# Second attention of a four-sublayer network: one transpose for two heads, and weights times values in four 64x64 tiles

## The chip, the cores and the metric

The kernel runs on one core of one Trainium2 chip. The metric is the device time of one execution in microseconds. Engines are named TensorE (PE in the profile, PEld for its loading of stationary operands), VectorE (DVE), ScalarE (ACT), GpSimd (POOL) and SyncE (SP). "Stationary" is the operand loaded into the array, "moving" the one that streams through it.

## The reference

The network has, one after the other, a mixture-of-experts layer, a causal attention, the mixture of experts again, a quantised gated layer, a second attention and the quantised layer again. Only the second attention is touched here. It attends over the first axis of its input, which has four entries, for 1024 columns and 16 heads of 64:

```
s, b, f = src.shape                      # 4, 1024, 128
qkv = jnp.einsum('sbf,pf->sbp', src, in_proj_weight) + in_proj_bias
q, k, v = jnp.split(qkv, 3, axis=-1)     # each 16 heads x 64
attn = jax.nn.softmax(jnp.einsum('nsd,ntd->nst', q / np.sqrt(d), k), axis=-1)
out = jnp.einsum('nst,ntd->nsd', attn, v)
out = out.reshape(s * b, h * d) @ out_proj_weight.T + out_proj_bias
x = x + out
```

So each token attends to only four tokens, those of its own column.

## The kernel before

`attention1_stage` is a software pipeline written by hand. The 4096 tokens are 32 tiles of 128; four tiles (QT) make a window w, so there are 8 windows. A tile of 128 tokens is 2 groups of 64 (index g), and a group holds 4 positions of 16 columns: attention never leaves a group of 64.

A unit of work is one slot i = 8w + r. There are 64 units, and the stages of a unit lie in different slots, by the constants `L_QK, L_S, L_TURN, L_V, L_PV, L_OUT = 0, 1, 11, 11, 12, 13`. In slot i TensorE does, in this order of program:

- QK (L1227 by L1236 and L1238): queries and keys of a pair of heads (128 rows) for a window of 512 tokens, into `pq` and `pk`. Each is three products of the split type fp32r (high times high, low times high, high times low).
- TURN (L1245): `pm`, the softmax weights of eight heads of one tile spread over a 64-wide pattern with zeros, is transposed into `pT`: eight transposes of 128x128. In `pm` (L1407, GpSimd) each head has 128 columns, 64 for g = 0 and 64 for g = 1, and `mask2` sets those of the other group to zero.
- V (L1227 by L1255): values of eight heads for one tile of 128 tokens, 512 columns, into `pV`; tokens are the stationary side (`xsh`, `xsl`).
- OUT (L1265): output projection of eight heads, four fp32 products of 128x128, from `ab` into `pO`. The hardware makes two passes of each fp32 product, so the profile counts eight.
- S (L1277): scores, eight fp32 products with 64 stationary columns, each into its half of the partitions of `pS`: 16 passes.
- PV (L1289): weights times values. Eight fp32 products, one for each head: 128 rows (tokens of both groups) by 64 stationary columns (`vb`), 128 moving columns (`pt`), even heads into partitions 0 to 63 of `pA`, odd heads into 64 to 127: 16 passes.

ScalarE copies `pq` to `qb` with the bias (L1304), `pT` to `pt` (L1313, 1024 columns), `pA` to `ab` (L1318, 512 columns). In every slot with r = 2 it then copies the window's part of `xh` and `xl` to `xsh` and `xsl` (L1323), on which V of the next slot waits by `x_copied`. VectorE writes `kz` (L1338, two instructions of 64 partitions; zeros stand beside the keys so that one product gives two heads), copies `pV` to `vb` (L1343), multiplies the scores by `mask16` (L1350), sums them (L1362), adds `pO` to the residual X (L1357), and does the softmax once in eight slots (L1369 to L1381). GpSimd expands the weights to `pm` (L1407, two instructions, one for each g). All waits are counts of semaphores written out by hand; `need` is a wait. Buffers `qb`, `kz`, `vb`, `pm` and `pt` are double, `ab` and the PSUM tiles single.

Of the kernel before, what the change touches and what calls it, by code (L numbers as in the profile page):

```python
# [10 lines left out]
P = 128  # L11
D = 128
# [1158 lines left out]
def attention1_stage(nc, C, name, load):  # L1171
# [6 lines left out]
    X, ident, xh, xl, mask16, mask2 = C["X"], C["ident"], C["xh"], C["xl"], C["mask16"], C["mask2"]  # L1178
# [7 lines left out]
    with Scope(nc, name) as s:  # L1186
        qb = [s.sb(f"qb{u}", [P, W]) for u in range(2)]
        kz = [s.sb(f"kz{u}", [P, 2, W]) for u in range(2)]
# [3 lines left out]
        xsh, xsl = s.sb("xsh", [P, W], F32R), s.sb("xsl", [P, W], F32R)  # L1192
# [25 lines left out]
        with nc.Block() as block:  # L1218
            @block.tensor
            def _(pe):  # L1220
# [8 lines left out]

                def slot(w, r, on):  # L1230
# [8 lines left out]
                    if on(L_TURN):  # L1239
                        j = i - L_TURN  # L1240
                        need(pe, expanded, 2 * (j + 1))
                        need(pe, t_kept, j)
                        m = pm[(r - L_TURN) % 2][:, :, :, :, :].rearrange("p h g t b -> p (h g t b)")
                        for hh in range(8):
                            last = nc.tensor.transpose(pT[:, hh * P:(hh + 1) * P], m[:, hh * P:(hh + 1) * P], ident[:, :])  # L1245
                        last.then_inc(t_ready, 1)
                    if on(L_V):
                        j = i - L_V
                        rr = (r - L_V) % 8
                        gp, u = rr // 2, rr % 2  # L1250

                        need(pe, x_copied, 2 * (w - (1 if r >= L_V - 8 else 2) + 1))
                        need(pe, v_kept, j)
                        c0 = 2 * INNER1 + u * 512
                        split3(pV[:, :], slice(c0, c0 + 512), xsh[:, gp * P:(gp + 1) * P], xsl[:, gp * P:(gp + 1) * P], True).then_inc(v_ready, 1)  # L1255
                    if on(L_OUT):
                        j = i - L_OUT
                        rr = (r - L_OUT) % 8
                        gp, u = rr // 2, rr % 2
                        need(pe, a_kept, j + 1)  # L1260
                        if u == 0:

                            need(pe, o_added, 4 * (w - (1 if r >= L_OUT - 8 else 2)) + gp)
                        for c in range(4):
                            last = mm(pO[:, 0:D], ab[:, c * P:(c + 1) * P], Wt["wo"][:, (4 * u + c) * D:(4 * u + c + 1) * D],  # L1265
                                      start=(u == 0 and c == 0), stop=(u == 1 and c == 3))
                        last.then_inc(o_done, 1)
                    if on(L_S):
# [5 lines left out]
                        for gp in range(QT):  # L1274
                            for g in range(2):
                                o = gp * P + g * 64
                                last = mm(pS[g * 64:(g + 1) * 64, gp * P:(gp + 1) * P].rearrange("p (a k) -> p a k", a=2),  # L1277
                                          qb[par][:, o:o + 64], kz[par][:, :, o:o + 64],
                                          start=True, stop=True)
                        last.then_inc(s_ready, 1)  # L1280
                    if on(L_PV):
                        j = i - L_PV
                        par = (r - L_PV) % 2
                        need(pe, t_kept, j + 1)
                        need(pe, v_kept, j + 1)
                        need(pe, a_kept, j)
# [9 lines left out]
            def _(act):  # L1296
                a = nc.scalar

                def slot(w, r, on):
# [14 lines left out]
                    if on(L_PV):  # L1314
# [12 lines left out]
            def _(dve):  # L1327
# [3 lines left out]
                def slot(w, r, on):  # L1331
                    i = 8 * w + r
                    if on(L_QK):
                        need(dve, k_ready, i + 1)
                        need(dve, s_ready, i - 1)
                        for par in range(2):
                            o = slice(64 * par, 64 * par + 64)
                            v.tensor_scalar(kz[r % 2][o, par, :], pk[o, :], Wt["bqk"][o, CH1 + r:CH1 + r + 1], None, ALU.add).then_inc(k_kept, 1)  # L1338
# [34 lines left out]
                    if r == 1 and on(2):  # L1373
# [5 lines left out]
                        if not isinstance(w, int) or w > 1:  # L1379
                            need(dve, expanded, 16 * (w - 1))  # L1380
                        v.tensor_tensor(Pn[:, :, :], Ec[:, :, :], b(ri), ALU.mult).then_inc(p_ready, 1)  # L1381
                for u in range(2):
                    v.memset(kz[u][:, :, :], 0.0).then_inc(zeroed, 1)
# [8 lines left out]
            def _(pool):  # L1392
# [3 lines left out]
                def slot(w, r, on):  # L1396
                    i = 8 * w + r
                    if on(LE):
# [7 lines left out]
                        for gg in range(2):  # L1406
                            g.tensor_tensor(pm[rr % 2][:, :, gg, :, :].rearrange("p h t b -> p h t b"),  # L1407
                                            src.rearrange("p (h t) -> p h t", t=SEQ1).unsqueeze(3).to_broadcast([P, 8, SEQ1, PER]),
                                            mask2[:, gg * PER:(gg + 1) * PER].unsqueeze(1).unsqueeze(1).to_broadcast([P, 8, SEQ1, PER]),
                                            ALU.mult).then_inc(expanded, 1)  # L1410
# [688 lines left out]
```

## Time and profile before

| | |
|---|---|
| median of 3 runs | 2016.22 us (2015.75 to 2020.72) |
| the profiled execution | 2022.96 us, span 2021.2 us |
| TensorE busy | 1651.2 us (82%) |
| VectorE busy | 1333.7 us (66%) |
| ScalarE busy | 932.3 us (46%) |
| GpSimd busy | 654.2 us (32%) |
| second attention | about 1468 to 1865 us of the span |

The profile is of one execution. "Busy" is the time in which an engine executed; the spans of products are drawn longer than their spacing, because they are pipelined, so the distance from one start to the next is what tells their cost. Line numbers (L1245) are those of the kernel before.

### The profile page before, as it was taken

Reading aid. Unit: us, or ns where it says so; the run is one execution under the profiler, and the core shown is the slowest. Engines: PE = TensorE matmul, PEld = TensorE weight load, DVE = VectorE, ACT = ScalarE, POOL = GpSimd, SP = SyncE. Lnnn points to the kernel's source line nnn. Section 1 sums busy time; section 2 is a strip of 40 time slices with the busy share of each in tenths; the row PEclk is TensorE's granted clock in tenths of the full one; section 3 lists DMA queues with packets and bytes.
Section 4 is the critical chain, followed back from the end, with each engine's and each line's share of the span. In section 5 each row is a group of like instructions: output and inputs, shape, how many; then the busy total and the mean of one; then the engine's idle time right before and its main releaser. Section 6 shows DMA issues by size and latency. Waiting matters only on the chain. (4 is left out here: it accounts for less than half of the span.)

```text
span 2021.2 us, 31502 instructions
## 1 busy us (share of the span) xinstructions
PE 1651.2 (82%) x10385; PEld 1169.7 (58%) x10385; DVE 1333.7 (66%) x2565; ACT 932.3 (46%) x1650; POOL 654.2 (32%) x797
## 2 busy tenths in 40 slices
PE   2997783899999999997499778277489999998575
PEld 2666671655555555554466666155358888887354
DVE  5633455988787888782553345699786666662896
ACT  2323341488887888884333333133224444444232
POOL 2486454211111111111268545133213333333132
PEclk9999996999999999999599889699699999999798
DMA  6022321111111111110512232100100000000000
GB/s 230 25 66 63 112 58 66 31 33 30 33 28 27 37 27 37 27 27 7 196 35 67 64 101 60 49 1 0 43 1 1 1 0 0 0 0 1 0 0 42
DMA packets 47705, 82.34 MB, mean 41 GB/s; under 512 B 10948, under 2 KB 32900, under 8 KB 46532
## 3 DMA queue, kind: packets, MB, share of 16 engines
q1 hardware_dynamic: 38500, 62.09, 10.7%
q0 software_dynamic: 9088, 18.76, 2.8%
q8 instruction: 65, 1.06, 0.2%
q14 instruction: 52, 0.43, 0.1%
HBM read 43.19 MB, written 31.22 MB: 37 GB/s over the span
## 5 line engine op out<-in xcount | busy, mean ns | idle before, releaser
L1861 DVE TENSOR_REDUCE z_parts<-z_pM 128x4 f32<-128x512 f32 x576 | 373.4, 685 | 94.7 <-PE z_pM L1601 92.6
L1778 ACT ACTIVATE z_Pr<-z_pE 128x512 f32<-128x512 f32 x576 | 322.5, 596 | 89.6 <-PE z_pE L1625 86.9
L1625 PE MATMUL z_pE<-z_QM,z_QK 128*128 128x512 f32 x576 | 250.9, 438 | 11.3 <-DMA z_QM<-z_Q 8.7
L1965 POOL TENSOR_SCALAR_AFFINE_SELECT z_Pr<-z_Pr 128x512 f32<-128x512 f32 x128 | 81.2, 635 | 483.6 <-ACT z_Pr L1778 483.6
L1601 PE MATMUL z_pM<-z_KM,z_Q 128*128 128x512 f32 x576 | 232.0, 407 | 1.8 <-DVE z_Q L1851 0.9
L1407 POOL TENSOR_TENSOR a_pm<-a_Pn,k_mask 128x512 f32<-128x512 f32 x128 | 132.2, 1057 | 271.4 <-PE a_pT L1245 153.2
L1625 PEld LDWEIGHTS z_pE<-z_QM,z_QK 128*128 128x128 f32 x576 | 107.9, 188 | 162.4 <-ACT z_Pr L1778 91.7
L466 POOL DMA_INDIRECT slot_results<-m_yq,m_xq x156 | 153.6, 985 | 146.0 <-ACT m_yq L664 117.7
L439 POOL DMA_INDIRECT slot_rows<-m_XN,m_dest x128 | 126.6, 989 | 108.5 <-DVE m_dest L747 73.2
L1638 PE MATMUL z_pO<-z_Pr,z_V 128*9 128x512 f32 (+3 forms) x1536 | 159.6, 489 | 0.1
L800 DVE TENSOR_TENSOR m_h<-m_sg,m_gu 128x512 f32<-128x512 f32 x78 | 53.6, 687 | 110.1 <-ACT m_sg L656 90.0
L1338 DVE TENSOR_SCALAR a_kz<-a_pk,s_bqk 64x512 f32<-64x512 f32 x128 | 95.9, 749 | 44.4 <-PE a_pk L1227 41.9
L1601 PEld LDWEIGHTS z_pM<-z_KM,z_Q 128*128 128x128 f32 x576 | 108.7, 189 | 18.6 <-DVE z_parts L1861 3.3
L1318 ACT ACTIVATE a_ab<-a_pA 128x512 f32<-128x512 f32 x64 | 38.3, 598 | 147.5 <-PE a_pA L1289 147.5
L656 ACT ACTIVATE m_sg<-m_gu 128x512 f32<-128x512 f32 x78 | 46.6, 598 | 119.0 <-PE m_gu L560 106.9
L700 DVE TENSOR_TENSOR m_h<-m_sg,m_gu 128x512 f32<-128x512 f32 x64 | 44.0, 688 | 69.4 <-PE m_gu L484 47.2
L560 PE MATMUL m_gu<-s_wh,m_xqh 128*128 x156 | 73.8, 473 | 19.3 <-issue 16.5
L1313 ACT ACTIVATE a_pt<-a_pT 128x1024 f32<-128x1024 f32 x64 | 65.6, 1026 | 45.7 <-PE a_pT L1245 45.7
L1350 DVE TENSOR_TENSOR a_md<-a_pS,k_mask 128x512 f32<-128x512 f32 x64 | 44.3, 692 | 62.2 <-PE a_pS L1277 61.8
L636 ACT ACTIVATE m_sg<-m_gu 128x512 f32<-128x512 f32 x64 | 38.1, 599 | 90.6 <-PE m_gu L480 75.9
L1098 PE MATMUL f_op<-s_wdT,f_hT 128*128 128x128 f32 x384 | 54.0, 293 | 30.7 <-ACT f_hT L1044 30.7
L493 PE MATMUL m_po<-m_h,s_w 128*128 128x512 f32 x128 | 67.7, 611 | 7.3 <-DVE m_h L700 7.3
(290 smaller groups left out, 3815.3 us busy)
## 6 DMA issues: line engine op xcount, KB each, us to landing
slot_rows<-in_c_pad SPq DMA_DIRECT2D x2, 5070.0 KB, 24.0
m_xq<-slot_rows SPq DMA_DIRECT2D x38, 260.0 KB
z_QM<-z_Q SPq DMA_DIRECT2D x128, 64.0 KB, 2.0
z_KM<-z_QK SPq DMA_DIRECT2D x60, 128.0 KB, 2.4
m_raw<-in_gu SPq DMA_DIRECT2D x2, 2048.0 KB, 8.7
m_XN<-slot_results SPq DMA_DIRECT2D x8, 512.0 KB, 7.0
m_raw<-slot_results SPq DMA_DIRECT2D x8, 512.0 KB, 5.1
slot_results<-m_yq,m_xq POOLq DMA_INDIRECT x156
```

Source lines behind the costliest of these rows:

```text
L439: g_.indirect_dma_start(xs_dram, bass.IndirectOffsetOnAxis(dest[:, k, t:t + 1], 0), XN[:, t, 2 - XO[k]:2 - XO[k] + ROW], None).then_inc(se ...
L466: g_.indirect_dma_start(y_dram, bass.IndirectOffsetOnAxis(xq[q % RING][:, j % QT, TAG[list_of(j)]:TAG[list_of(j)] + 1].bitcast(I32), 0), y ...
L493: mm(po[:, :], w2[:, o:o + D], h[n % 2][:, :], start=(i == 0), stop=(i == NCHUNK - 1)).then_inc(h_used, 1)
L560: last = mm(gu[r % 2][:, u, :], xv[q % 2][:, c], wt[:, bass.ds(es[u] * GU, GU)], start=a, stop=b)
L1338: v.tensor_scalar(kz[r % 2][o, par, :], pk[o, :], Wt["bqk"][o, CH1 + r:CH1 + r + 1], None, ALU.add).then_inc(k_kept, 1)
L1407: g.tensor_tensor(pm[rr % 2][:, :, gg, :, :].rearrange("p h t b -> p h t b"), src.rearrange("p (h t) -> p h t", t=SEQ1).unsqueeze(3).to_br ...
L1601: last = mm(pM[n % 3][:, :].rearrange("p (h k) -> p h k", h=4), Q[G % 2][:, qt * P:(qt + 1) * P], KM[G % 2][:, :, kb * P:(kb + 1) * P], st ...
L1625: mm(pE[e % 2][:, :].rearrange("p (h c) -> p h c", h=4), QK[G % RING][:, kt * P:(kt + 1) * P], QM[half][:, :, q * P:(q + 1) * P], start=Tr ...
L1638: last = mm(pO[32 * h:32 * h + DH0 + 1, lo:512], V[:, (G // 4) * KT + kt, 4 * (G % 4) + h, :], Pr[j % 4][:, h, lo:512], start=(kt == 0), s ...
L1778: a.activation(Pr[j % 4][:, :, q * P:(q + 1) * P], pE[e % 2][:, :].rearrange("p (h c) -> p h c", h=4), ACT.Exp, scale=DH0 ** -0.5).then_in ...
L1861: v.tensor_reduce(parts[:, qt, kb, :], pM[n % 3][:, :].rearrange("p (h k) -> p h k", h=4), AX.X, ALU.max).then_inc(maxed, 1)
L1965: g_.affine_select(blk, blk, [[0, 4], [1, P]], ALU.is_ge, 0.0, base=0, channel_multiplier=-1).then_inc(selected, 1)
```

## The change

The softmax weights of a head are no longer spread over 128 columns with zeros for the other group. `pm` has 64 columns a head, so a transpose of 128 columns turns two heads side by side: four transposes instead of eight, one GpSimd instruction instead of two, and `pt` and `pT` are half as wide. After the transpose the even head of a pair lies in partitions 0 to 63 and the odd head in 64 to 127, for g = 0 in columns 0 to 63 and g = 1 in 64 to 127. To make the contraction rows fit, the scores of g = 1 have odd and even head exchanged (new layout of `kz`), and the values of odd heads are computed with the two halves of the tokens exchanged: `xsh` and `xsl` get 192 columns a tile, the last 64 a copy of the first, and V becomes two times three products of 256 columns. PV becomes sixteen products of 64 rows by 64 stationary columns with 64 moving columns, in the four 64x64 tiles of the array; the two halves of rows write to two PSUM tiles `pA[0]` and `pA[1]`. `ab` is filled by four copies of 64x256 instead of one of 128x512. The waits of PV stand ahead of S.

```diff
-        pm = [s.sb(f"pm{u}", [P, 8, 2, SEQ1, PER]) for u in range(2)]
-        pt = [s.sb(f"pt{u}", [P, 8 * P]) for u in range(2)]
-        ab = s.sb("ab", [P, 4 * P])
-        pq, pk, pS, pV, pA, pO = (s.ps(n, [P, 512]) for n in ("pq", "pk", "pS", "pV", "pA", "pO"))
-        pT = s.ps("pT", [P, 1024])
+        pm = [s.sb(f"pm{u}", [P, 8, SEQ1, PER]) for u in range(2)]
+        pt = [s.sb(f"pt{u}", [P, 4 * P]) for u in range(2)]
+        ab = s.sb("ab", [P, 4, 2, 64])
+        pq, pk, pS, pV, pT, pO = (s.ps(n, [P, 512]) for n in ("pq", "pk", "pS", "pV", "pT", "pO"))
+        pA = [s.ps(f"pA{u}", [P, 512]) for u in range(2)]
...
+                def values(out, u, odd, x_hi, x_lo):
+                    cols = lambda wt: wt[:, 2 * INNER1 + u * 512:2 * INNER1 + (u + 1) * 512].rearrange("p (i k c) -> p i k c", k=2, c=DH1)[:, :, odd, :]
+                    mm(out, x_hi, cols(Wt["wh"]), start=True, stop=False)
+                    mm(out, x_lo, cols(Wt["wh"]), start=False, stop=False)
+                    return mm(out, x_hi, cols(Wt["wl"]), start=False, stop=True)
...
-                        for hh in range(8):
+                        for hh in range(4):
                             last = nc.tensor.transpose(pT[:, hh * P:(hh + 1) * P], m[:, hh * P:(hh + 1) * P], ident[:, :])
...
-                        split3(pV[:, :], slice(c0, c0 + 512), xsh[:, gp * P:(gp + 1) * P], xsl[:, gp * P:(gp + 1) * P], True).then_inc(v_ready, 1)
+                        for odd in range(2):
+                            xr = slice(64 * odd, 64 * odd + P)
+                            last = values(pV[:, odd * 256:(odd + 1) * 256].rearrange("p (i c) -> p i c", c=DH1), u, odd, xsh[:, gp, xr], xsl[:, gp, xr])
+                        last.then_inc(v_ready, 1)
...
+                    if on(L_PV):
+                        j = i - L_PV
+                        need(pe, t_kept, j + 1)
+                        need(pe, v_kept, j + 1)
+                        need(pe, a_kept, 4 * j)
                     if on(L_S):
...
-                        for hh in range(8):
-                            h0 = (hh % 2) * 64
-                            last = mm(pA[h0:h0 + 64, (hh // 2) * P:(hh // 2 + 1) * P], vb[par][:, hh * 64:(hh + 1) * 64],
-                                      pt[par][:, hh * P:(hh + 1) * P], start=True, stop=True)
+                        for c in range(4):
+                            for g in range(2):
+                                for odd in range(2):
+                                    half = (g + odd) % 2
+                                    rows, o = slice(64 * half, 64 * half + 64), odd * 256 + c * 64
+                                    last = mm(pA[half][64 * odd:64 * odd + 64, c * 64:(c + 1) * 64], vb[par][rows, o:o + 64],
+                                              pt[par][rows, c * P + g * 64:c * P + g * 64 + 64], start=True, stop=True)
...
-                        a.activation(ab[:, :], pA[:, :], ACT.Copy).then_inc(a_kept, 1)
+                        for half in range(2):
+                            for odd in range(2):
+                                rows = slice(64 * odd, 64 * odd + 64)
+                                a.activation(ab[rows, :, (half + odd) % 2, :], pA[half][rows, 0:256].rearrange("p (c k) -> p c k", c=4), ACT.Copy).then_inc(a_kept, 1)
...
-                            a.activation(dst[:, :], src[:, bass.ds((w - 1) * W, W)].bitcast(F32), ACT.Copy).then_inc(x_copied, 1)
+                            of = src[:, bass.ds((w - 1) * W, W)].bitcast(F32).rearrange("p (g k) -> p g k", g=QT)
+                            a.activation(dst[:, :, 0:P], of, ACT.Copy).then_inc(x_copied, 1)
+                            a.activation(dst[:, :, P:P + 64], of[:, :, 0:64], ACT.Copy).then_inc(x_copied, 1)
...
-                            v.tensor_scalar(kz[r % 2][o, par, :], pk[o, :], Wt["bqk"][o, CH1 + r:CH1 + r + 1], None, ALU.add).then_inc(k_kept, 1)
+                            v.tensor_scalar(kz[r % 2][o, :, par:4 - par:3 - 2 * par, :], pk[o, :].rearrange("p (n g k) -> p n g k", n=QT, g=2), Wt["bqk"][o, CH1 + r:CH1 + r + 1], None, ALU.add).then_inc(k_kept, 1)
...
-                        for gg in range(2):
-                            g.tensor_tensor(pm[rr % 2][:, :, gg, :, :].rearrange("p h t b -> p h t b"),
...
+                        g.tensor_tensor(pm[rr % 2][:, :, :, :], src.rearrange("p (h t) -> p h t", t=SEQ1).unsqueeze(3).to_broadcast([P, 8, SEQ1, PER]),
+                                        mask16[:, :].unsqueeze(1).unsqueeze(1).to_broadcast([P, 8, SEQ1, PER]), ALU.mult).then_inc(expanded, 1)
```

The counts in the other waits follow (`expanded` one instead of two a unit, `a_kept` four instead of one, `x_copied` four instead of two a window).

## Rows read from the trace of the kernel before

**Rows 1.** The page's first part: busy time, share of the span, instructions.

```profile
PE 1651.2 (82%) x10385; PEld 1169.7 (58%) x10385; DVE 1333.7 (66%) x2565; ACT 932.3 (46%) x1650; POOL 654.2 (32%) x797
```

**Rows 2.** Stretches, full slots and tail: us; PE, PEld, DVE, ACT, POOL busy; PEclk; DMA.

```profile
1515.12:1818.43 303.31, 303.31 (x2909) 265.98 (x2907) 196.97 (x311) 125.94 (x171) 105.43 (x102) 1.00 0.00 0
1818.43:1865.00 46.57, 44.46 (x435) 39.04 (x433) 13.35 (x25) 20.27 (x27) 18.61 (x18) 1.00 0.01 1
```

**Rows 3.** Order of time, one full slot on PE: start, length, line, operation.

```profile
1604.35 0.50 PE L1227 MATMUL a_pq<-s_xh,s_wh 128*128 x1
...
1605.15 0.40 PE L1227 MATMUL a_pk<-s_xh,s_wh 128*128 x1
...
1605.85 1.03 PE L1245 MATMUL a_pT<-k_ident,a_pm 128*128 128x128 f32 x8
1606.64 0.48 PE L1227 MATMUL a_pV<-s_wh,a_xsh 128*128 128x512 f32 x1
...
1607.42 1.05 PE L1265 MATMUL a_pO<-s_wo,a_ab 128*128 128x128 f32 x8
1608.40 1.09 PE L1277 MATMUL a_pS<-a_kz,a_qb 128*64 128x128 f32 x16
1609.33 1.04 PE L1289 MATMUL a_pA<-a_pt,a_vb 128*64 128x128 f32 x16
1610.30 0.50 PE L1227 MATMUL a_pq<-s_xh,s_wh 128*128 x1
```

**Rows 4.** Order of time, first attention: 128-column products of the split type.

```profile
378.37 0.28 PE L1585 MATMUL z_pE<-s_wh,s_xl 128*128 128x128 f32 x1
378.48 0.28 PE L1585 MATMUL z_pE<-s_wl,s_xh 128*128 128x128 f32 x1
```

**Rows 5.** Order of time, first attention: eight passes in four column tiles.

```profile
502.74 0.41 PE L1638 MATMUL z_pO<-z_Pr,z_V 128*9 128x128 f32 x8
503.07 0.50 PE L1625 MATMUL z_pE<-z_QM,z_QK 128*128 128x512 f32 x1
```

**Rows 6.** Order of time on DVE, the slot after a softmax; [idle before <-releaser].

```profile
1597.65 0.69 DVE L1350 TENSOR_TENSOR a_md<-a_pS,k_mask 128x512 f32<-128x512 f32 x1 [0.90 <-PE a_pS L1277]
```

**Rows 7.** Groups by form: busy us, mean ns of one, idle before.

```profile
L1313 ACT ACTIVATE a_pt<-a_pT 128x1024 f32<-128x1024 f32 x64 | 65.6, 1026 | 45.7 <-PE a_pT L1245 45.7
L1033 ACT ACTIVATE f_xT<-f_txp 128x256 f32<-128x256 f32 x32 | 12.3, 384 | 59.9 <-PE f_txp L1072 59.9
L1308 ACT ACTIVATE a_Ec<-a_Dc 128x256 f32<-128x256 f32 x8 | 3.3, 417 | 1.3 <-DVE a_Dc L1372 1.3
L1407 POOL TENSOR_TENSOR a_pm<-a_Pn,k_mask 128x512 f32<-128x512 f32 x128 | 132.2, 1057 | 271.4 <-PE a_pT L1245 153.2 <-DVE a_Pn L1381 118.2
```

**Rows 8.** Order of time, the slot r = 3 of a window (with copies of x).

```profile
1598.52 0.60 ACT L1318 ACTIVATE a_ab<-a_pA 128x512 f32<-128x512 f32 x1 [2.47 <-PE a_pA L1289]
1599.02 0.62 ACT L1323 ACTIVATE a_xsh<-s_xh 128x512 fp32r x1
1599.54 0.62 ACT L1323 ACTIVATE a_xsl<-s_xl 128x512 fp32r x1
```

**Rows 9.** Order of time on PE in the tail, starts of groups.

```profile
1825.56 1.09 PE L1289 MATMUL a_pA<-a_pt,a_vb 128*64 128x128 f32 x16
...
1827.43 0.48 PE L1227 MATMUL a_pV<-s_wh,a_xsh 128*128 128x512 f32 x1
...
1829.20 1.09 PE L1289 MATMUL a_pA<-a_pt,a_vb 128*64 128x128 f32 x16
1830.23 1.09 PE L1245 MATMUL a_pT<-k_ident,a_pm 128*128 128x128 f32 x8
1832.03 0.50 PE L1227 MATMUL a_pV<-s_wh,a_xsh 128*128 128x512 f32 x1 [0.71 <-ACT a_xsl L1323]
...
1859.32 1.09 PE L1289 MATMUL a_pA<-a_pt,a_vb 128*64 128x128 f32 x16
1861.12 1.16 PE L1265 MATMUL a_pO<-s_wo,a_ab 128*128 128x128 f32 x8 [0.70 <-ACT a_ab L1318]
```

More of the change, by code:

```diff
@@ L1187, in attention1_stage @@
         qb = [s.sb(f"qb{u}", [P, W]) for u in range(2)]
-        kz = [s.sb(f"kz{u}", [P, 2, W]) for u in range(2)]
+        kz = [s.sb(f"kz{u}", [P, QT, 4, 64]) for u in range(2)]
         md = s.sb("md", [P, 4 * 2 * SEQ1, PER])
@@ L1191, in attention1_stage @@
         mx, sm, ri = (s.sb(n, [P, QT * HEADS1]) for n in ("mx", "sm", "ri"))
-        xsh, xsl = s.sb("xsh", [P, W], F32R), s.sb("xsl", [P, W], F32R)
+        xsh, xsl = s.sb("xsh", [P, QT, 3 * 64], F32R), s.sb("xsl", [P, QT, 3 * 64], F32R)
         vb = [s.sb(f"vb{u}", [P, W]) for u in range(2)]
-        pm = [s.sb(f"pm{u}", [P, 8, 2, SEQ1, PER]) for u in range(2)]
-        pt = [s.sb(f"pt{u}", [P, 8 * P]) for u in range(2)]
-        ab = s.sb("ab", [P, 4 * P])
-        pq, pk, pS, pV, pA, pO = (s.ps(n, [P, 512]) for n in ("pq", "pk", "pS", "pV", "pA", "pO"))
-        pT = s.ps("pT", [P, 1024])
+        pm = [s.sb(f"pm{u}", [P, 8, SEQ1, PER]) for u in range(2)]
[3 more added lines that the diff above has]
+        pA = [s.ps(f"pA{u}", [P, 512]) for u in range(2)]
         q_ready, k_ready, q_kept, k_kept, s_ready, masked, reduced = (
@@ L1250, in slot @@
                         gp, u = rr // 2, rr % 2
-                        need(pe, x_copied, 2 * (w - (1 if r >= L_V - 8 else 2) + 1))
+                        need(pe, x_copied, 4 * (w - (1 if r >= L_V - 8 else 2) + 1))
                         need(pe, v_kept, j)
-                        c0 = 2 * INNER1 + u * 512
-                        split3(pV[:, :], slice(c0, c0 + 512), xsh[:, gp * P:(gp + 1) * P], xsl[:, gp * P:(gp + 1) * P], True).then_inc(v_ready, 1)
+                        for odd in range(2):
+                            xr = slice(64 * odd, 64 * odd + P)
+                            last = values(pV[:, odd * 256:(odd + 1) * 256].rearrange("p (i c) -> p i c", c=DH1), u, odd, xsh[:, gp, xr], xsl[:, gp, xr])
+                        last.then_inc(v_ready, 1)
                     if on(L_OUT):
@@ L1259, in slot @@
                         gp, u = rr // 2, rr % 2
-                        need(pe, a_kept, j + 1)
+                        need(pe, a_kept, 4 * (j + 1))
                         if u == 0:
@@ L1264, in slot @@
                         for c in range(4):
-                            last = mm(pO[:, 0:D], ab[:, c * P:(c + 1) * P], Wt["wo"][:, (4 * u + c) * D:(4 * u + c + 1) * D],
+                            last = mm(pO[:, 0:D], ab[:, c, :, :].rearrange("p g k -> p (g k)"), Wt["wo"][:, (4 * u + c) * D:(4 * u + c + 1) * D],
                                       start=(u == 0 and c == 0), stop=(u == 1 and c == 3))
                         last.then_inc(o_done, 1)
+                    if on(L_PV):
[3 more added lines that the diff above has]
+                        need(pe, a_kept, 4 * j)
                     if on(L_S):
@@ L1283, in slot @@
                         par = (r - L_PV) % 2
-                        need(pe, t_kept, j + 1)
-                        need(pe, v_kept, j + 1)
-                        need(pe, a_kept, j)
-                        for hh in range(8):
-                            h0 = (hh % 2) * 64
-                            last = mm(pA[h0:h0 + 64, (hh // 2) * P:(hh // 2 + 1) * P], vb[par][:, hh * 64:(hh + 1) * 64],
-                                      pt[par][:, hh * P:(hh + 1) * P], start=True, stop=True)
+                        for c in range(4):
[5 more added lines that the diff above has]
+                                              pt[par][rows, c * P + g * 64:c * P + g * 64 + 64], start=True, stop=True)
                         last.then_inc(pv_ready, 1)
```

15 lines of the change are left out of this document (6 added, 9 removed).

## The prediction

> **What bounds the kernel now.** I read the engines' totals, then the busy times by stretch, then the order of time inside one slot. Over the whole kernel TensorE is busy 82% [rows 1], a mean over stages with different limits, so the stage decides. Its steady part is 51 equal slots (i = 13 to 63) from 1515.12 to 1818.43 us: TensorE is busy 303.31 of 303.31 us, at a granted clock of 1.00 (the 2.4 GHz level), VectorE 197 us, ScalarE 126 us [rows 2]. One slot takes 1610.30 - 1604.35 = 5.95 us, and TensorE works through it in the order pq, pk, pT, pV, pO, pS, pA without an idle gap [rows 3]. So a slot costs what its groups cost, start to start:
>
> pq 0.80, pk 0.70, pT 0.79, pV 0.78, pO 0.98, pS 0.93, pA 0.97, together 5.95 us [rows 3].
>
> Two things inside these numbers are needed below. A 128x128 load with a 128-column product takes 0.11 us: eight transposes in 0.79, eight pO passes in 0.98 less 0.10. Where the array goes from 128x128 to 128x64 or back, about 0.10 us is lost ahead of it (pO: 0.98 against 8 x 0.11; pA: 0.97 against eight pairs at 0.109, 0.87), and the first load behind it is not hidden (pq 0.80 against pk 0.70; pS 0.93 against 0.87) [rows 3]. pA already runs in two column tiles: 16 passes of 128 columns in 8 pairs.
>
> The Trainium skill (TensorEngine Tiling, "Key Properties") says that a change of the tiling mode drains the engine; by that rule the new step from 128x64 (pS) to 64x64 (pA) costs as much as the ones above, and I charge 0.10 for it. It speaks against this change; without it the slot would be 0.10 shorter.
>
> **The change, part by part, on TensorE.**
> TURN: four transposes instead of eight, 4 x 0.11 = 0.44 less: pT 0.35.
> V: three products of 512 columns become six of 256. Three of 512 take 0.70 in pk, 0.233 each [rows 3], so 256 columns are 0.115. The bound by the weights is 0.11: full loads with 128-column products of this split type come every 0.11 us [rows 4]. Both say 6 x 0.115 = 0.69, and 0.69 is what three of 512 are in pV too (0.78 less 0.09 for a first product that is charged longer). Taken: 0.78 unchanged (0.75 to 0.85).
> OUT and S keep instruction counts and shapes. S's new layout of keys only makes its moving rows contiguous: nothing. S is followed by a change of mode: pS 0.93 + 0.10 = 1.03.
> PV: 16 products in two passes each, 32 passes of 64 rows by 64 columns in four tiles. Between the ends: if all four tiles run at once, 8 rounds of 64 columns at 0.109/2 = 0.055 are 0.44, with 0.05 for the first load and 0.10 for the change of mode 0.59 us. If the two halves of rows don't run beside each other, or loads of 64 columns aren't hidden behind products of 64, it is 16 steps of 0.055, 0.87 + 0.15 = 1.02. No operation with 64 rows is in the trace. The nearest row is the first attention's pO: eight passes in four column tiles, 128 columns, 0.33 us start to start with the change behind it, so two rounds of 0.11 and not eight [rows 5]. Four tiles in parallel are shown, row halves are not. I take 0.59.
> The waits of PV are moved ahead of S. They ask for t_kept, v_kept and a_kept of the slot before, all a slot old or needed by OUT already, so S does not wait for them. Cost nothing.
> New slot: 0.80 + 0.70 + 0.35 + 0.78 + 0.98 + 1.03 + 0.59 = 5.23, 0.72 us less.
>
> **On the other engines.** VectorE: the same instructions (the two writes of kz get another stride, the element count stays); in the fullest slot (softmax) it still waits 0.90 us for pS ahead of md [rows 6], more than the slot loses, 0.72. Cover just holds. GpSimd: one instruction of 1.06 us instead of two [rows 7], hidden before and after. ScalarE: pt is 128x512 instead of 128x1024, near the 0.60 of pA's copy instead of 1.03 [rows 7, 8]. But pA's copy becomes four of 64x256. A copy of 256 from PSUM lasts 0.384 [rows 7]; back to back, copies start about 0.10 before the one ahead ends (0.60 long, 0.50 apart; 0.62 long, 0.52 apart) [rows 8], so 0.28 each and 1.24 for four instead of 0.60. In a full slot OUT needs them 2.63 us in: hidden.
>
> **Where that cover is gone.** Once in 8 slots ScalarE copies xsh and xsl between ab and qb. Before: ab starts 0.11 into slot r=3 (1598.52 against 1598.41), xsl ends at 1600.16, 1.75 in; V starts 2.29 in [rows 3, 8] and doesn't wait. After: ab from 0.11, four steps of 0.284 to 1.25, then 0.52 and 0.31 (256 from SBUF: 0.417 [rows 7] less 0.10) for xsh, 0.52 and 0.41 for xsl: x_copied at 3.01, with 0.05 for the semaphore 3.06. V would start at 0.80 + 0.70 + 0.35 = 1.85. TensorE stands still 1.2 us, with OUT, S and PV queued behind that wait. Bounds: 1.0 (64 rows cheaper) to 1.8 (no overlap of the copies). Six of the 51 slots are such slots.
>
> **Head and tail of the stage.** Slots 0 to 10 have no changed group. Slots 11 and 12 gain 0.44 and 0.72. In the tail (no pq, pk) a slot is 3.64 us (1829.20 - 1825.56), of it pA 1.03 (1830.23 - 1829.20) and pT 0.84 (1827.43 - 1825.56 less 1.03) [rows 9]. After: pT 0.41 (0.84 less four times 0.11) and pV 0.78 end at 1.19, but OUT now waits for the four copies, 0.22 + 1.24 = 1.46; then pO 0.98, pA 0.65 (0.59, and 0.06 that pA has more in the tail now, 1.03 against 0.97): 3.09, 0.55 less in eight slots, 4.4 us; slot 64 (with S) 0.45 less. The slot with the x copies: V starts at 3.06 instead of 1.80 (1832.03 against 1830.23, a wait of this kind is there already [rows 9]) and is 0.84 longer. The last two distances from PV to OUT, 1.79 (0.97 for pA, 0.60 for the copy, 0.22 between) [rows 9], become 0.59 + 1.46 = 2.05, 0.26 more each; one of them stands against a turn that is 0.22 shorter. Net tail: 4.4 + 0.45 - 0.84 - 0.3 = 3.7.
>
> **Sum.** 51 x 0.72 = 36.7; slots 11 and 12 1.2; x copies 6 x 1.2 = 7.2 lost; tail 3.7: 34.4 us less. The profiled execution took 2022.96 (span 2021.2), the median of the three runs is 2016.22; the sum is a difference inside the span and nothing around it moves, so I take it from the median: 2016.2 - 34.4 = 1981.8, say 1982.
>
> **Rivals.**
> (a) Row halves in turn, or loads not hidden: PV 1.02 instead of 0.59. 0.43 x 64 = 27.5 more: 2009. For it: no row with 64 rows. Against: column tiles run side by side both in loads and products [rows 3, 5]. Chance 0.09.
> (b) A floor for each matmul, whatever its width. From rows: the eight passes in 0.33 less 0.10 are 0.029 apart on average [rows 5], so nothing denser is shown over a group; 32 x 0.029 + 0.15 = 1.08 at the worst, 0.49 more than taken, at the best nothing. Halfway (0.022 each, 0.85) it is 0.26 x 64 = 17 more: 1999. Chance 0.12.
> The Trainium skill (TensorE: Matmul & The Clock Gate, "Wait — 56ns, not 53.3ns?") states such a floor: start to start never below about 25 ns. Estimate from that page: 32 x 0.025 = 0.80, PV 0.95, about 2005. No row here settles whether it holds across tiles; rows 5 show eight passes within 0.33 us.
> (c) Slower: instructions can't be supplied. Load and product count each. Per slot TensorE executes (2909 + 2907) / 51 = 114 now [rows 2]; the densest stretch is pS and pA, 64 in 1.90 us, 0.030 each [rows 3]. After, the same stretch has 96 in 1.62 us, 0.017 each. If 0.030 is the sustained limit, it takes 2.88, 1.26 more: the slot is 6.49, 0.54 longer than before; in the tail 64 x 0.030 is 1.92 for PV, 1.33 more than taken in 12 slots, 16 less the gain of 3.7. 51 x 0.54 + 7.2 + 12 = 47 more than before: 2063. It decides from 0.023 an instruction ((1.62 + 0.58) / 96; 0.58 is the slot's gain after its share of the x copies, 7.2 / 51). Against it: the 0.030 is explained by the columns alone. Chance 0.07.
> (d) ScalarE's small copies cost more, or VectorE's cover of 0.18 us in the softmax slots fails: x stalls of 1.8 and half a us in two slots of eight, 4 + 6 = 10 more: 1992. Chance 0.10.
> That the change doesn't do what it says: half the transposes and half of GpSimd's instructions go in any case, so this is (a).
>
> **How the numbers follow.** Forecast 1982: chance 0.62, its own range 1973 (S to PV without the 0.10, stalls of 1.0) to 1990. (a) 0.09, (b) 0.12, (c) 0.07, (d) 0.10. Range 1972 to 2006: it takes in the forecast, (d) and (b), together 0.84; (a) and (c) stay outside. A measurement of this kernel can tell about 0.3%, 6 us, from no change. Faster by more, under 2010: forecast, (d), nearly all of (b) and most of (a): 0.88. Within: 0.05. Slower: 0.07.
>
> **What would show it.** pT 0.35 and pV 0.78 start to start; pS 1.03 and pA 0.59 (0.59 right, 0.85 to 1.08 rival b, 1.02 rival a, 1.9 rival c); slot 5.23; a_ab's four copies 0.28 apart; in six slots TensorE idle about 1.2 us ahead of pV, released by ScalarE's a_xsl; in the tail a short wait of pO for a_ab. The prediction is wrong if pA's group is over 0.9 us, if TensorE waits in ordinary slots for VectorE or ScalarE, or if the granted clock in the stage falls from 1.00.

## The result and the profile after

The changed kernel takes 2001.71 us (median of 4; 2000.59 to 2003.37) against 2016.85 for the kernel before: ratio 0.9926, 95% interval 0.9911 to 0.9941, so 12 to 18 us faster. On a second chip it was 0.9911 (0.9888 to 0.9934). The forecast was 1982, with 1972 to 2006 as the range. The kernel is faster, as forecast, and the time lies inside the range, but the gain is 15 us where 34 were forecast.

The page of the profiled execution of the changed kernel: totals, then the groups on ScalarE and GpSimd that the change touches.

```profile
PE 1617.2 (81%) x11340; PEld 1139.1 (57%) x11345; DVE 1333.3 (67%) x2565; ACT 963.5 (48%) x1858; POOL 589.2 (29%) x733
...
L1343 ACT ACTIVATE a_ab<-a_pA 64x256 f32<-64x256 f32 x256 | 96.9, 379 | 151.4 <-PE a_pA L1311 146.7
L1433 POOL TENSOR_TENSOR a_pm<-a_Pn,k_mask 128x512 f32<-128x512 f32 x64 | 67.3, 1057 | 312.8 <-PE a_pT L1258 191.0
```

TensorE is 34 us less busy, GpSimd 65, and ScalarE 31 more: one copy of 0.60 (64 of them, 38.3 us) has become four of 0.379 (96.9 us), while the copy of `pT` to `pt` fell from 1.03 to 0.59. Lines have moved: TURN is now L1258, V L1239 to L1241, OUT L1280, S L1298, PV L1311, the copies of pA L1343.

One full slot on TensorE in the changed kernel, order of time:

```profile
1517.23 0.50 PE L1232 MATMUL a_pq<-s_xh,s_wh 128*128 128x512 f32 x1
...
1518.05 0.40 PE L1232 MATMUL a_pk<-s_xh,s_wh 128*128 128x512 f32 x1
...
1518.75 0.60 PE L1258 MATMUL a_pT<-k_ident,a_pm 128*128 128x128 f32 x4
1519.10 0.37 PE L1239 MATMUL a_pV<-s_wh,a_xsh 128*128 128x256 f32 x1
...
1519.88 1.05 PE L1280 MATMUL a_pO<-s_wo,a_ab 128*128 128x128 f32 x8
1520.86 1.09 PE L1298 MATMUL a_pS<-a_kz,a_qb 128*64 128x128 f32 x16
1521.89 0.70 PE L1311 MATMUL a_pA<-a_pt,a_vb 64*64 64x64 f32 x32
1522.51 0.50 PE L1232 MATMUL a_pq<-s_xh,s_wh 128*128 128x512 f32 x1
```

From start to start, beside [rows 3]: pq 0.82 (0.80), pk 0.70 (0.70), pT 0.35 (0.79), pV 0.78 (0.78), pO 0.98 (0.98), pS 1.03 (0.93), pA 0.62 (0.97). The slot is 5.28 us instead of 5.95, the forecast said 5.23.

The stretches that answer to [rows 2]: the 51 full slots, then the tail up to the last pO.

```profile
1511.98:1792.22 280.24, 271.10 (x3677) 234.40 (x3672) 196.65 (x311) 149.72 (x336) 53.70 (x51) 1.00 0.00 0
1792.22:1842.00 49.78, 39.26 (x615) 34.21 (x607) 13.50 (x26) 28.42 (x68) 9.45 (x9) 0.92 0.01 2
```

TensorE is no longer busy all of the time: 9.1 us are missing in the full slots. The sum of the prediction, part by part, against the two profiled executions (differences of starts of the first pq, of slots 13 and 64 and of the last pO; us):

| part | before | forecast | after |
|---|---|---|---|
| slots 0 to 12 | 46.6 | -1.2 | 45.6 (-1.0) |
| 51 full slots | 303.3 | -29.5 | 280.3 (-23.1) |
| tail to the last pO | 45.6 | -3.7 | 49.7 (+4.1) |
| the stage | 395.5 | -34.4 | 375.5 (-20.0) |

Ahead of the stage lie 1468.5 and 1466.4 us, behind its last pO 157.2 and 159.7 us. In ten other executions of this study the time ahead was anything between 1460.4 and 1473.9 us, whatever the second attention did, while the parts of the stage repeated within 0.2 us between the two executions of the changed kernel. The stage's own parts are therefore the measure below, and medians the check. The 2.5 us more behind the last pO are taken up under "The medians".

Where the 9.1 us went: a slot with r = 3, in order of time, both engines.

```profile
1543.63 0.50 PE L1232 MATMUL a_pq<-s_xh,s_wh 128*128 x1
...
1543.77 1.59 ACT L1343 ACTIVATE a_ab<-a_pA 64x256 f32<-64x256 f32 x4 [2.49 <-PE a_pA L1311]
...
1545.15 0.60 PE L1258 MATMUL a_pT<-k_ident,a_pm 128*128 128x128 f32 x4
...
1545.39 0.63 ACT L1349 ACTIVATE a_xsh<-s_xh 128x512 fp32r x1
...
1545.92 0.40 ACT L1350 ACTIVATE a_xsh<-s_xh 128x256 fp32r x1
1546.23 0.61 ACT L1349 ACTIVATE a_xsl<-s_xl 128x512 fp32r x1
1546.75 0.40 ACT L1350 ACTIVATE a_xsl<-s_xl 128x256 fp32r x1
...
1547.20 0.39 PE L1239 MATMUL a_pV<-s_wh,a_xsh 128*128 128x256 f32 x1 [1.45 <-ACT a_xsl L1350]
```

This is the wait that the prediction named, with its price wrong: pV starts 2.05 us after pT instead of 0.35, so 1.70 us are lost, not 1.2 (the whole slot takes 7.00 us, 1.72 more than 5.28). The prediction's upper bound for this wait, 1.8, was the one for copies that do not overlap. The copies of x behave as forecast (0.53, 0.31, 0.52 from start to start); the four copies of pA take 1545.39 - 1543.77 = 1.62 up to the start of the next copy, not 1.14.

The tail, order of time on TensorE:

```profile
1800.65 0.37 PE L1239 MATMUL a_pV<-s_wh,a_xsh 128*128 128x256 f32 x1
...
1802.01 1.16 PE L1280 MATMUL a_pO<-s_wo,a_ab 128*128 128x128 f32 x8 [0.42 <-ACT a_ab L1343]
1803.10 0.69 PE L1311 MATMUL a_pA<-a_pt,a_vb 64*64 64x64 f32 x32
1803.72 0.66 PE L1258 MATMUL a_pT<-k_ident,a_pm 128*128 128x128 f32 x4
1807.28 0.58 PE L1239 MATMUL a_pV<-s_wh,a_xsh 128*128 128x256 f32 x1 [2.90 <-ACT a_xsl L1350]
...
1837.40 1.73 PE L1280 MATMUL a_pO<-s_wo,a_ab 128*128 128x128 f32 x8 [1.70 <-ACT a_ab L1343]
```

From pV to pO are 1.36 us (0.78 before), and pO itself is 1.09 long, because its first load stands behind a wait. The slot with the x copies has pV 3.56 us behind pT. After this idle time TensorE's granted clock is lower:

```profile
1804.00:1812.00 8.00, 5.10 (x57) 4.57 (x56) 0.69 (x1) 4.38 (x11) 1.05 (x2) 0.79 0.00 0
1836.00:1844.00 8.00, 4.87 (x48) 4.16 (x48) 0.00 (x0) 2.79 (x8) 0.00 (x0) 0.61 0.00 0
```

Behind the wait of 2.90 us the mean over 8 us is 0.79, and the products of 256 columns start 0.21 us apart where they had been 0.115. Behind the last waits for `ab` it is 0.61.

### The profile page after: what moved, and what is told of

Same layout as the page of the kernel before. It is cut to its first block and busy times, and to the rows that moved or that the text cites. A ratio compares the mean times of both kernels' runs of the same rounds, so it can differ in the third digit from the quotient of the medians.

```text
span 2001.6 us, 33649 instructions
## 1 busy us (share of the span) xinstructions
PE 1617.2 (81%) x11340; PEld 1139.1 (57%) x11345; DVE 1333.3 (67%) x2565; ACT 963.5 (48%) x1858; POOL 589.2 (29%) x733
## 5 line engine op out<-in xcount | busy, mean ns | idle before, releaser
L1343 ACT ACTIVATE a_ab<-a_pA 64x256 f32<-64x256 f32 x256 | 96.9, 379 | 151.4 <-PE a_pA L1311 146.7
L1433 POOL TENSOR_TENSOR a_pm<-a_Pn,k_mask 128x512 f32<-128x512 f32 x64 | 67.3, 1057 | 312.8 <-PE a_pT L1258 191.0
L656 ACT ACTIVATE m_sg<-m_gu 128x512 f32<-128x512 f32 x78 | 46.6, 597 | 120.8 <-PE m_gu L560 120.8
L1280 PE MATMUL a_pO<-s_wo,a_ab 128*128 128x128 f32 x512 | 70.9, 283 | 7.6 <-ACT a_ab L1343 7.6
L1791 ACT ACTIVATE z_pM<-k_after_query 128x512 f32<-128x512 bf16 x120 | 72.6, 605 | 0.6 <-DVE z_parts L1885 0.5
```

What stands on the lines that cost most here:

```text
L1343: a.activation(ab[rows, :, (half + odd) % 2, :], pA[half][rows, 0:256].rearrange("p (c k) -> p c k", c=4), ACT.Copy).then_inc(a_kept, 1)
L1791: a.activation(pM[n % 3][:, :], after_query[:, :], ACT.Copy).then_inc(filled, 1)
```

## Experiments

The theory after reading the trace: TensorE's own sum is right, and what is missing is ScalarE. The four copies of 64x256 are not overlapped and end late; this makes V wait once a window, and OUT wait in each slot of the tail. Rivals: the x wait only hides another one; the number of copies does not matter; the four tiles are not what made PV short.

### x copies ahead of the copies of pA

```diff
+                    if r == L_V - 9 and on(L_V - 1):
+                        ...
+                            a.activation(dst[:, :, 0:P], of, ACT.Copy).then_inc(x_copied, 1)
+                            a.activation(dst[:, :, P:P + 64], of[:, :, 0:64], ACT.Copy).then_inc(x_copied, 1)
                     if on(L_PV):
...
-                    if r == L_V - 9 and on(L_V - 1):
-                        ...
```

> The changed kernel with one edit: in the slot r = 2 ScalarE copies xsh and xsl after pt and ahead of the copies of pA, not behind them. Theory (the loss against the forecast is the wait of V for x_copied, and in the tail what hangs on it): the wait of 1.72 us ahead of pV goes in all six full slots, 51 full slots take 280.3 - 10.3 = 270 us, the slot with the x copies in the tail falls from 7.48 to about 3.5 us, no stretch of the tail is at the lower clock; in all 14 us less than the changed kernel, about 1987. Rival (the x copies only move the wait: now they hold up the copies of pA, and OUT waits): the wait reappears ahead of pO and less than 4 us is gained, about 1999.

Measured: 1982.72 us against 2020.30 of the kernel before on this chip, ratio 0.9824 (0.9802 to 0.9846). The stretches of full slots and tail:

```profile
1506.44:1776.27 269.83, 269.46 (x3679) 234.10 (x3673) 196.63 (x311) 149.87 (x336) 53.80 (x51) 1.00 0.00 0
1776.27:1821.23 44.96, 36.79 (x612) 31.91 (x607) 13.47 (x26) 28.24 (x68) 9.46 (x9) 1.00 0.01 2
```

The full slots lose 10.4 us and TensorE is busy all but 0.4 us; the tail loses 4.7 and its clock is 1.00 throughout. The slot with the x copies in the tail takes 3.75 us (7.48 before the edit). The stage takes 360.3 us, 15.2 less than in the changed kernel, where 14 were expected. The theory stands and the rival falls: nothing waits in ordinary slots in place of V. The copies fit into time in which ScalarE had waited for pA, behind pt:

```profile
1535.16 0.59 ACT L1335 ACTIVATE a_pt<-a_pT 128x512 f32<-128x512 f32 x1
1535.76 0.63 ACT L1341 ACTIVATE a_xsh<-s_xh 128x512 fp32r x1
...
1537.12 0.40 ACT L1342 ACTIVATE a_xsl<-s_xl 128x256 fp32r x1
1538.23 1.59 ACT L1350 ACTIVATE a_ab<-a_pA 64x256 f32<-64x256 f32 x4 [0.72 <-PE a_pA L1311]
```

### The same edit in the kernel before

The edit is as above, with the two copies of 512 columns ahead of the one copy of pA.

> The kernel before with the one edit that helped the changed kernel: x copies ahead of the copy of pA. Theory (the wait in the full slots is made by the change; before, x_copied was 0.5 us early): full slots stay 303.3 us, the tail loses its one wait of 0.96 us, 44.6 instead of 45.6. Rival (the order helps any version by making the copy of pA or of pq fall better): the full slots fall under 302.

Measured: full slots 303.32 us, tail 44.59 (45.57 before the edit); one execution of 2019.22 us, the kernel before on this chip 2015.47 in the median. The order of the copies gains nothing in the full slots of the kernel before, and the 1.0 us of its one wait in the tail. So the wait in full slots is made by the change.

### Four copies in the kernel before

```diff
-                        a.activation(ab[:, :], pA[:, :], ACT.Copy).then_inc(a_kept, 1)
+                        for half in range(2):
+                            for odd in range(2):
+                                rows, cols = slice(64 * odd, 64 * odd + 64), slice(256 * half, 256 * half + 256)
+                                a.activation(ab[rows, cols], pA[rows, cols], ACT.Copy).then_inc(a_kept, 1)
```

> The kernel before with one part of the change alone: pA is copied to ab by four instructions of 64x256 instead of one of 128x512. Theory (copies of 64x256 don't overlap, 1.61 us in all): x_copied comes at 2.92 in its slot, V waits 0.6 us in six full slots, in the tail pO waits 0.2 us a slot, the last two distances from PV to OUT grow by 1.0 each: 3.7 + 2 + 2 + 1 = about 9 us slower, 2026. Rival (they overlap as forecast, 0.28 apart): x_copied at 2.4, 0.1 to 0.2 us in six slots and 1.3 at the end, 2 to 3 us slower, 2019.

Measured: 2027.02 us, ratio 1.0036 (1.0022 to 1.0051). Full slots 307.39 us (+4.1), tail 51.64 (+6.1). In its slot r = 3 pV starts 1.43 us after pT, 0.64 later than before, which is the 0.6 expected. In the stage this one part of the change costs the kernel before some 10 us (6.7 by the medians, 2027.02 against 2020.30), and the price without overlap is the right one: with overlap 2 to 3 us were expected.

### Two copies of 64x512

The counts in the waits for `ab` follow (two instead of four).

```diff
-        pA = [s.ps(f"pA{u}", [P, 512]) for u in range(2)]
+        pA = s.ps("pA", [P, 2, 512])
...
-                        for half in range(2):
-                            for odd in range(2):
-                                rows = slice(64 * odd, 64 * odd + 64)
-                                a.activation(ab[rows, :, (half + odd) % 2, :], pA[half][rows, 0:256]...
+                        for odd in range(2):
+                            rows = slice(64 * odd, 64 * odd + 64)
+                            dst = ab[rows, :, :, :] if odd == 0 else ab[rows, :, ::-1, :]
+                            a.activation(dst.rearrange("p c g k -> p g c k"), pA[rows, :, 0:256].rearrange("p h (c k) -> p h c k", c=4), ACT.Copy).then_inc(a_kept, 1)
```

> The changed kernel with pA as one tensor of two banks and two copies of 64x512 into ab instead of four of 64x256. Theory (each copy costs 0.40 us from start to start, its length and a gap of 0.02, none of it overlapped): two copies of 0.62 are 1.24 instead of 1.61, the wait ahead of pV falls from 1.72 to about 1.35, pV to pO in the tail from 1.36 to about 1.0; 6 x 0.37 + 12 x 0.37 = 6.6 us less than the changed kernel, about 1995. Rival (64-wide copies overlap once they are 512 long, as the 128-wide did, 0.50 apart): 1.10 for both, about 1993. Rival (the cost is by partitions and elements alone, the number of copies doesn't matter): no gain, 2002.

Measured: 1992.80 us, ratio 0.9863 (0.9839 to 0.9887). A copy is 0.592 long and the next starts 0.62 after its start: no overlap at 512 columns either (second copy and what follows, order of time on ScalarE):

```profile
1544.68 0.59 ACT L1343 ACTIVATE a_ab<-a_pA 64x512 f32<-64x512 f32 x1
1545.30 0.63 ACT L1349 ACTIVATE a_xsh<-s_xh 128x512 fp32r x1
```

Full slots 277.81 us (-2.4), tail 43.62 (-6.1), pV to pO in the tail 0.99. The full slots gain what was expected (6 x 0.37 = 2.2); the tail gains more than 12 x 0.37 = 4.4, and its mean granted clock is 0.96 instead of 0.92. So the number of copies matters: two of 512 columns take 1.23 us to the start of what follows, four of 256 take 1.62.

### Two copies of all 128 partitions

The four copies become two of 128x256, from pA[0] and pA[1]. The exchange of groups for odd heads is left out, so this kernel computes another attention and only its times are of use.

> The changed kernel with two copies of 128x256 from pA[0] and pA[1] into ab instead of four of 64x256; the exchange of the two groups for odd heads is left out, so the second attention's result is another one. It tells what forbids the overlap. If it is the 64 partitions: the two copies start 0.28 to 0.30 us apart. If it is the short length, 256 elements out of PSUM: they start 0.40 apart. In both cases the pair ends 0.8 to 0.9 us earlier than the four did, so the wait ahead of pV falls to about 0.9 and the total to about 1990.

Measured: the pair takes 0.66 us, each 0.38 long, so the second starts 0.28 after the first:

```profile
1545.83 0.66 ACT L1341 ACTIVATE a_ab<-a_pA 128x256 f32<-128x256 f32 x2 [2.59 <-PE a_pA L1311]
```

With 256 columns out of PSUM copies do overlap, if they are 128 wide. The wait ahead of pV is 0.63, where 0.9 was expected. The full slots take 273.73 us (-6.5) and the tail 37.57 (-12.1). The one execution took 1990.74 us, as expected, but with 1473.9 us ahead of the stage, the most of all. But the two copies of 64 differ from these in two things, in having 64 partitions and in changing them. The next run parts the two.

### The same four copies in another order

```diff
-                        for half in range(2):
-                            for odd in range(2):
+                        for odd in range(2):
+                            for half in range(2):
```

> The changed kernel with the order of the four copies of 64x256 changed: both of partitions 0 to 63, then both of 64 to 127. What forbids the overlap? If it is the change of partitions from one copy to the next: the first and second, and the third and fourth, start 0.28 us apart, the second and third 0.40; V's wait falls by 0.24. If it is that a copy has 64 partitions at all: all 0.403 apart, the same time as the changed kernel.

Measured: 1988.51 us in one execution; full slots 278.50 (-1.8), tail 45.12 (-4.6). The four copies together:

```profile
1544.36 1.32 ACT L1343 ACTIVATE a_ab<-a_pA 64x256 f32<-64x256 f32 x4 [2.43 <-PE a_pA L1311]
1545.71 0.69 ACT L1326 ACTIVATE a_qb<-a_pq,s_bqk 128x512 f32<-128x512 f32 x1
```

They take 1.32 us instead of 1.59: starts at 0.28, 0.67 and 0.96 after the first. So 64 partitions do not forbid the overlap. Going to other partitions than the copy ahead does; there 0.39 pass between the starts. It is not the PSUM tile that decides: the pairs that overlap here read one from pA[0] and one from pA[1], while in the changed kernel the first two copies read the same tile and do not overlap. Whether it is the partitions read or the partitions written stays open, as both change together. The stage takes 369.1 us, 6.2 less than in the changed kernel on this chip; the rest of the difference between the totals lies outside it. The order in the changed kernel alternates between partitions 0 to 63 and 64 to 127 at each step, the worst there is.

The Trainium skill (ScalarE: Activation LUTs, "What ACT_TABLE_LOAD costs") says that ACTIVATEs back to back overlap by about 93 ns. That agrees with the copies of equal partitions here (0.38 long, 0.28 apart). For a change of partitions the measurement decides: no overlap.

### PV tile by tile

```diff
-                        for c in range(4):
-                            for g in range(2):
-                                for odd in range(2):
+                        for g in range(2):
+                            for odd in range(2):
+                                for c in range(4):
```

> The changed kernel with the sixteen products of PV in another order: all four of one tile of the array, then the next tile, instead of one product for each of the four tiles in turn. Theory (the four tiles run beside each other only where products for different tiles stand next to each other in the queue; passes of one tile follow at 0.0585 us): 32 passes take 1.87 us, pA's group 2.0 instead of 0.62, a slot 6.65 instead of 5.28, and the total about 70 + 18 = 88 us more, near 2090. Rival (the array reorders, or the row halves do not matter and a pass is simply 0.0146 us): pA's group stays at 0.62.

Measured: 2050.92 us in one execution, 31 us over the kernel before on this chip (2020.08). Order of time on TensorE:

```profile
1559.49 1.54 PE L1311 MATMUL a_pA<-a_pt,a_vb 64*64 64x64 f32 x32
1560.95 0.50 PE L1232 MATMUL a_pq<-s_xh,s_wh 128*128 x1
```

The same 32 passes take 1.46 us instead of 0.62. So the four tiles are what made PV short, row halves included, and only because neighbours in the queue belong to different tiles. The 2.0 expected was too much, and with it the 88 us: the passes of two tiles that follow each other in the queue still overlap in part. The full slots take 321.47 us, 41 more, and the whole stage 51 more, so the order of these loops decides whether the change gains or loses.

### Both edits, and the changed kernel again beside them

> The changed kernel with both edits: x copies ahead of the copies of pA, and two copies of 64x512 instead of four of 64x256. Theory (the two losses are separate: the x wait in six full slots and one of the tail, the copies in every slot of the tail): 51 full slots 269.8 us as with the first edit alone, the tail 44.96 less 12 x 0.37 = 40.5 us, so some 4.5 us less than with the first edit alone and 14 to 15 less than the changed kernel in the stage's own time. Rival (the gains of the two edits overlap, both work on the same wait): no more than 1 us under the first edit alone, tail at 44.

> The changed kernel unaltered, on the same chip as the run with both edits, to compare the two and to see how much of the time lies outside the stage. Theory: the stage's parts repeat (0 to 12: 45.6, 13 to 63: 280.3, tail 49.7 us within 0.3), while the time ahead of the stage differs by some us from one execution to the next. Rival: the parts of the stage vary too, and the differences read between traces are partly chance.

Measured on one chip, the kernel before 2020.08: the changed kernel 2002.53, ratio 0.9911 (0.9888 to 0.9934); with both edits 1981.16, ratio 0.9804 (0.9782 to 0.9826). The parts of the changed kernel repeat (45.5, 280.3, 49.5 us). With both edits the full slots and the tail are:

```profile
1508.27:1778.03 269.76, 269.44 (x3678) 234.01 (x3673) 196.67 (x311) 137.92 (x234) 53.83 (x51) 1.00 0.00 0
1778.03:1818.07 40.04, 36.80 (x612) 31.91 (x607) 13.48 (x26) 23.94 (x42) 9.47 (x9) 1.00 0.01 2
```

The gains add: the tail is another 4.9 us shorter than with the first edit alone, where 4.5 was expected. By the ratios alone (0.9824 and 0.9804, intervals overlapping) the second edit could not be told from nothing; the parts of the stage show it. The stage takes 355.3 us, 40 less than before the change, where the changed kernel has 20 less.

### One of the two copies on VectorE

```diff
+                    if on(L_PV):
+                        j = i - L_PV
+                        need(dve, pv_ready, j + 1)
+                        need(dve, o_done, j)
+                        v.tensor_copy(ab[64:128, :, ::-1, :].rearrange("p c g k -> p g c k"), pA[64:128, :, 0:256].rearrange("p h (c k) -> p h c k", c=4)).then_inc(b_kept, 1)
                     if r == 0 and on(1):
```

> The kernel with both edits, and one more: of the two copies of 64x512 out of pA ScalarE keeps the one of partitions 0 to 63, VectorE takes the other, behind its sum of the scores in the same slot. Theory (in the tail pO waits for the copies alone: 0.99 us from pV to pO, 1.09 for pO and 2.02 from pA to pO twice): with both copies side by side 0.78, 0.98 and 1.4; the tail falls from 40.0 to about 35.5 us, the full slots keep 5.28 (269.8 us), near 1977. Rival (VectorE, busy 197 of 280 us and in order, becomes late in the slots with the softmax): TensorE waits for VectorE in full slots, over 272 us for the 51, and nothing is gained.

Measured: 1976.70 us, ratio 0.9813 (0.9789 to 0.9837) against 2015.47 on its chip, within the interval of both edits alone.

```profile
1508.16:1779.90 271.74, 270.92 (x3678) 234.48 (x3673) 233.78 (x362) 108.36 (x183) 53.82 (x51) 1.00 0.00 0
1779.90:1817.48 37.58, 34.34 (x612) 31.38 (x607) 22.61 (x39) 15.97 (x29) 9.45 (x9) 1.00 0.01 2
```

Both sides were half right: the tail gains 2.5 us, and the full slots lose 2.0, one slot in eight growing from 5.28 to 5.60 (5.76 once), where VectorE's copy comes late behind the softmax. The profile names no releaser for that wait of pO; the copy ends at 1585.29 and the first load of pO starts at 1585.53, so the copy as its cause is inferred from the times. The sum is 0.5 us. The version with both edits is simpler and as good.

## Why the prediction was right or wrong

**TensorE's sum: right.** pT 0.35, pV 0.78, pO 0.98 and pS 1.03 came as forecast, the last with the 0.10 for the new change of tiling mode; in that the trace agrees with the rule of the Trainium skill (TensorEngine Tiling, "Key Properties") that was cited. pA is 0.62 for 0.59, and pq 0.82 for 0.80. Together 0.05 a slot, 2.6 us in 51.

**Rival (a), row halves in turn: false.** pA would be 1.02; the run tile by tile shows what a lack of concurrency costs. **Rival (b), a floor for each pass: false** across tiles. 32 passes in 0.62 us, with 0.15 for the mode in it, are 0.015 each. The floor of 0.025 that the Trainium skill states (TensorE: Matmul & The Clock Gate, "Wait — 56ns, not 53.3ns?") would have given 0.80 for the passes alone; across tiles the measurement decides. **Rival (c), supply of instructions: false** as a price for each slot. It may show in one place: in the last slot of a turn of TensorE's loop, five times in the 51 slots, pA to pq takes 0.76 to 0.81 instead of 0.62.

```profile
1615.21 0.69 PE L1311 MATMUL a_pA<-a_pt,a_vb 64*64 64x64 f32 x32
1616.02 0.49 PE L1232 MATMUL a_pq<-s_xh,s_wh 128*128 x1
```

Before, the same place took 0.97 like any other. That the branch and the register instructions of the loop are no longer hidden behind a PV that is so short is the likely cause. The run tile by tile speaks for it: with as many instructions in the loop and a PV of 1.46 us, these slots are as long as the others (6.10). It was not tried by itself. The slots behind them are a little shorter, so that it costs 0.7 us in all.

**The step that failed** is the sentence "back to back, copies start about 0.10 before the one ahead ends ..., so 0.28 each". It carried an overlap over from rows of 128 partitions [rows 8] to copies that change partitions, where it is not there: 0.403 each. The mechanism (V waits for x_copied, OUT waits in the tail) was right, the term was mis-sized: 1.59 us for the four instead of 1.24. The run with the same four copies in another order shows that the change of partitions is what it missed. In the full slots 1.72 us were lost instead of 1.2, six times 0.52 = 3.1 us; with 2.6 for the slots and 0.7 for the loop that makes the 6.4 us that are missing there.

**The tail, +4.1 instead of -3.7,** failed by the same term and two that were not in the sum. From start to start (us):

- The copies, 4.3: pV to pO is 1.36 instead of 1.05 in ten slots (3.1), V starts 3.56 behind pT instead of 3.06 in the slot with the x copies (0.5), and the last two distances from pA to pO are 0.35 longer each for them (0.7).
- A pO whose first load stands behind a wait is 1.09 long, not 0.98, eleven times: 1.2. The first full wait of that kind could be read in the kernel before (1.16 for the group in [rows 9] against 1.05 in [rows 3]) and was not charged.
- The fallen clock, 2.5: behind its V the slot with the x copies takes 3.92 instead of 2.40 (7.48 in all instead of 5.46), and at the end a pO takes 1.66 instead of 1.09 and the last distance is 2.84 instead of 2.40. In the run with two wide copies, whose clock stays at 1.00 through the tail, the first of these places takes 2.41; with the x copies ahead, at 1.00 too, the other two take 1.09 and 2.40.

Together 8.0, where 7.8 are missing. The prediction put the clock at nothing without a reason, though it had named a fall from 1.00 as a sign of being wrong; the mean of the tail is 0.92. So of the 14.4 us by which the stage falls short of its forecast, the mis-sized copies are 7.4, half. Rival (d) held the right engine and nearly the right wait (1.8), but priced only the full slots.

That the time lies inside the range is partly luck: the upper end stood at 2006 for the sake of rival (b), which is false, and rival (d), the one that came nearest to what happened, stood at 1992.

**VectorE's and GpSimd's cover held:** in full slots of the changed kernel TensorE waits for nobody but ScalarE's x copies.

**The medians.** The forecast took the difference from the median and held that nothing around the stage moves. The stage moved by 20.0 us, the medians by 15.1, the second chip's by 17.6. 2.5 to 3 us more lie behind the stage (157.2 before, 159.7 and 160.3 in the changed kernel, 157.3 with both edits). The last pO is 0.9 us longer at the lower clock, but that is made up again: 24.3 us behind it both kernels are level (1888.29 - 1864.00 and 1866.21 - 1841.90, starts of the same transposes of the next layer). The difference comes later in that layer, where TensorE's granted clock differs. Here are 30 to 45 us behind the last pO, first the kernel before, then the changed one:

```profile
1894.00:1909.00 15.00, 9.53 (x38) 6.46 (x39) 12.98 (x17) 3.55 (x8) 4.64 (x6) 0.89 0.00 0
1871.90:1886.90 15.00, 9.52 (x33) 6.27 (x34) 11.79 (x15) 3.60 (x8) 4.33 (x5) 0.77 0.01 1
```

Each of the twelve profiled executions has one of these two values. The six with 0.89 took 157.2 to 158.4 us behind the last pO, the six with 0.77 took 157.8 to 160.3; among the latter is the kernel before with its x copies ahead. So the changed kernel was at the lower value both times, but not it alone, and what decides between them is open. So is the rest of the distance between 20.0 and 15.1; it is small beside the 13.5 us by which the time ahead of the stage varies.

## What to carry to other kernels

A change that takes a ninth off the bottleneck's slot (5.95 to 5.28 us) shortens the cover of all other engines, and any extra work it puts on one of them is then priced at the place where that engine works through a queue that something waits for: here once in eight slots and in the tail, 15 us in all, given back by moving four instructions. Walk each engine's queue through the rare slots too, and through the drain of the pipeline. Where products are small, order them so that neighbours in the queue belong to different tiles of the array, and where copies are small, so that neighbours work on the same partitions.

## What the runs showed of the hardware

- ScalarE: a copy starts about 0.10 us before the one ahead ends if both work on the same partitions (0.28 apart at 0.38 long, with 64 or with 128), and 0.02 after its end if the partitions change (0.403 at 0.378 long; 0.62 at 0.592 long). A copy of 64 partitions is as long as one of 128 (0.378 and 0.382).
- Equal partitions are not always enough: in the changed kernel the copy to `qb` behind the last x copy, both of 128 partitions, starts 0.425 after it at 0.399 long (1546.75 and 1547.17). In the run with two wide copies the same pair is 0.31 apart at 0.41 long. This was not followed up.
- TensorE: 32 fp32 passes of 64 rows by 64 columns with 64 moving columns, a tile each in turn, take 0.62 us with the changes of mode; run tile by tile 1.46.
- TensorE's clock: in the tail of the changed kernel, behind a wait of 2.90 us and again behind waits of 1.70, products ran at the lower level, 1.2 GHz, for part of the time (means of 0.79 and 0.61 over 8 us; 0.21 instead of 0.115 us for 256 columns). With the x copies ahead, and that wait gone, the mean of the whole tail was 1.00.
